# Releasing a group's row gathers in four runs of two instead of one run of eight

## The reference, cut to what matters

```
row, col = (edge_index[0], edge_index[1])
out = jnp.concatenate([x[row], edge_attr], axis=1)
out = jax.nn.selu(out @ W1a + b1a) @ W1b + b1b
summed = jax.ops.segment_sum(out, col, num_segments=x.shape[0])
counts = jax.ops.segment_sum(jnp.ones((out.shape[0],), out.dtype), col, num_segments=x.shape[0])
mean = summed / jnp.maximum(counts, 1.0)[:, None]
h = jnp.concatenate([x, mean, u[batch]], axis=1)
return jax.nn.selu(h @ W2a + b2a) @ W2b + b2b
```

## Time and profile before

| what | value |
|---|---|
| median of three runs | 3514.62 us (3498.83 to 3517.24) |
| the profiled execution | 3513.92 us, span 3512.1 us |
| mean granted TensorE clock | 0.782 of full speed |
| busy share: PE, PEld, DVE, ACT, POOL | 67%, 47%, 44%, 29%, 52% |
| DMA queue of POOL (q0) | 54240 packets, 57.23 MB, 7.5% of 16 engines |
| chain that ended last, by kind | PE 36%, another core or an unknown queue 25%, issue 22%, DVE 6%, ACT 5% |

### The profile page before, as it was taken

How to read it: one execution, slowest core, us unless ns; L and a number is a source line. 1 busy time by engine, 2 the same in 40 slices (tenths; PEclk the granted TensorE clock), 3 DMA queues, 4 the chain that set the end, 5 groups by cost and what they waited for, 6 DMA issues and landing times.

```text
span 3512.1 us, 52018 instructions
## 1 busy us (share of the span) xinstructions
PE 2340.6 (67%) x18382; PEld 1666.3 (47%) x18382; DVE 1547.9 (44%) x3098; ACT 1005.2 (29%) x2255; POOL 1824.9 (52%) x1853
## 2 busy tenths in 40 slices
PE   3999999787888862565656566565656656564643
PEld 1555565444444431454544455454545545453543
DVE  6899998233333441333433333343333334332333
ACT  4778776000000011222222222222222222222222
POOL 6366763555455557454444545444554544455552
PEclk9999999888888875677777777777767777676566
DMA  6658877649455521322222222222222222221111
GB/s 227 196 196 241 224 210 253 175 119 219 143 173 176 176 68 40 83 48 44 46 48 43 48 46 48 44 46 48 43 48 46 48 44 46 48 42 42 39 37 34
DMA packets 478172, 346.45 MB, mean 99 GB/s; under 512 B 357844, under 2 KB 428687, under 8 KB 474253
## 3 DMA queue, kind: packets, MB, share of 16 engines
q1 hardware_dynamic: 367443, 272.49, 27.4%
q0 software_dynamic: 54240, 57.23, 7.5%
q10 hardware_dynamic: 56250, 13.52, 1.9%
HBM read 200.58 MB, written 142.39 MB: 98 GB/s over the span
## 4 chain that ended last, share of the span: by engine, by line
PE 36%; another core or an unknown queue 25%; issue 22%; DVE 6%; ACT 5%; DMA 2%; SPq 2%; DVEq 1%; ACTq 1%; POOL 0%; POOLq 0%
PE agg_ps L1533 5%; PE u_ps L1664 4%; PE cnt_ps L1404 4%; PE cnt_ps L1625 3%; PE agg_ps L1410 3%; PE agg_ps L1411 3%; PE u_ps L1660 2%; PE agg_ps L1674 2%; PE agg_ps L1633 2%; ACT A_sb L1071 2%; PE t_ps L1617 1%; PE v_ps L1650 1%; DVEq L2192 1%; ACT A_sb L1217 1%
## 5 line engine op out<-in xcount | busy, mean ns | idle before, releaser
L976 POOL DMA_INDIRECT A_sb<-source_terms,src_cur x1172 | 1118.5, 954 | 1048.4 <-ACT src_cur L1203 718.1
L927 POOL DMA_INDIRECT sorted_edges<-pm_row,pm_to x440 | 482.7, 1097 | 338.8 <-DVE pm_to L1981 215.5
L1664 PE MATMUL u_ps<-arena 128*128 128x64 bf16 x3399 | 253.4, 212 | 385.5 <-issue 385.2
L1533 PE MATMUL agg_ps<-A_sb,arena 128*128 128x448 f16 x1911 | 426.1, 373 | 68.7 <-issue 65.7
L1857 DVE TENSOR_TENSOR arena<-iota_code,arena 128x2048 f16<-128x2048 f16 (+1 forms) x392 | 438.3, 1186 | 33.5 <-PE cnt_ps L1404 31.2
L1071 ACT ACTIVATE A_sb<-cnt_ps 128x392 f32 (+1 forms) x784 | 386.0, 499 | 123.4 <-PE cnt_ps L1404 73.0
L1664 PEld LDWEIGHTS u_ps<-arena 128*128 128x128 bf16 x3399 | 196.7, 110 | 439.9 <-issue 431.9
L2194 DVE TENSOR_TENSOR A_sb<-A_sb,agg_ps 65x48 f32 (+1 forms) x290 | 78.0, 269 | 728.7 <-remote 624.4
L1533 PEld LDWEIGHTS agg_ps<-A_sb,arena 128*128 128x128 bf16 x1911 | 189.5, 101 | 274.0 <-issue 133.0
L1404 PE MATMUL cnt_ps<-arena 128*128 128x98 f16 x3136 | 282.2, 214 | 31.2 <-ACT A_sb L1071 23.2
L1633 PE MATMUL agg_ps<-A_sb 128*65 128x48 f32 x2344 | 210.9, 250 | 131.4 <-issue 73.4
(11 more groups left out here) (308 smaller groups left out, 3379.3 us busy)
## 6 DMA issues: line engine op xcount, KB each, us to landing
counts_matrix<-A_sb SPq DMA_DIRECT2D x14, 5488.0 KB
A_sb<-counts_matrix SPq DMA_DIRECT2D x12, 5488.0 KB
arena<-in_edge_attr_dram SPq DMA_DIRECT2D x96, 256.0 KB
sorted_edges<-zrow SPq DMA_DIRECT2D x11, 1716.0 KB
A_sb<-source_terms,src_cur POOLq DMA_INDIRECT x1172
arena<-sorted_edges SPq DMA_DIRECT2D x143, 128.0 KB
overlapping_rows<-A_sb SPq DMA_DIRECT2D x1, 13056.0 KB, 39.4
A_sb<-in_edge_attr_dram SPq DMA_DIRECT2D x50, 256.0 KB
```

The lines of the kernel that those rows point to most:

```text
L927: pool.indirect_dma_start(out=sorted_d, out_offset=bass.IndirectOffsetOnAxis(ap=pm_to[:, k, j:j + 1], axis=0), in_=pm_row[:, k, j, :], in_ ...
L976: pool.indirect_dma_start(out=gath[k][:, j * F:(j + 1) * F], out_offset=None, in_=p_d, in_offset=bass.IndirectOffsetOnAxis(ap=src_cur[k][: ...
L1533: ins = pe.matmul(agg_ps[:, 0:SBN], Hsb[:, part, blk, :], Asb(half)[:, blk, :], start=False, stop=(part == 2), skip_group_check=True)
L1664: ins = pe.matmul(u_ps[:, j * F:(j + 1) * F], lane_p[u % 2][:, a, j * P:(j + 1) * P], P3[:, 2 * b + a, part, :], start=False, stop=(part = ...
```

## The change

POOL still issues the same 8 gathers for a group, from the same indices into the same buffer, and in the same order. But now it issues them in four runs of two, and waits ahead of each:

1. as before, for `z_made` of group g-6 and `idx_made` of group g;
2. for `attr_turned` of group g-4, which PE turns in slot g-6;
3. for `seg_ready` of group g-6: the window sums of slot g-6, the last thing PE does in that slot apart from units;
4. for `z_made` of group g-5, the DVE's next `add_terms`.

The last group has half the width and so gets four runs of one gather. The first six groups stay as they were.

```diff
-            def gather(g, k, width=EJ):
-                for j in range(width):
+            def gather(g, k, first=0, end=EJ):
+                for j in range(first, end):
                     pool.indirect_dma_start(
...
                 pool.wait_ge(z_made, g - DEEP + 1)
                 pool.wait_ge(idx_made, g + 1)
                 pool.sem_inc(pool_at, 1)
-                gather(g, k, width)
+                gather(g, k, 0, width // 4)
+                pool.wait_ge(attr_turned, g - DEEP + 3)
+                pool.sem_inc(pool_at, 1)
+                gather(g, k, width // 4, width // 2)
+                pool.wait_ge(seg_ready, g - DEEP + 1)
+                pool.sem_inc(pool_at, 1)
+                gather(g, k, width // 2, 3 * width // 4)
+                pool.wait_ge(z_made, g - DEEP + 2)
+                pool.sem_inc(pool_at, 1)
+                gather(g, k, 3 * width // 4, width)
```

## The result

The changed kernel takes 3286.14 us (median of 4 runs, 3275.39 to 3290.11), the kernel before 3515.93 us beside it (4 runs, 3498.83 to 3527.1). The ratio is 0.9346, 95% interval 0.93 to 0.9391.

The account below looks back on a forecast made before the run. The prediction took the edge stage as bound by gather bursts and the engines' work, which hardly overlap. From 3513.9 us, -46 for 112 slots and -16 for the last slots gave 3452 us; own range 3405 to 3495, 8 in 10 3310 to 3600.

Parts of the forecast that it names:

- What holds everything back: Edge stage: bursts of gathers slow all other engines, from 63% of the free pace in 3 us to 8% late.
- the shared-interface reading: DVE and GpSimd contend for SBUF interfaces, so the loss would lie inside DVE's instructions, however the gathers are cut.
- The 6 us more of slow time for a group cut in four: Estimate from the skill's fixed DMA cost of about 2.0 us; the prediction's own rows gave 3 x 0.85.
- Added waits at 0: POOL's three new waits a group: satisfied ones cost nothing; others, restarting 0.83 us after the event, also counted 0.
- The cut: Edge stage: how the runs merge; a period's 32 gathers, before in bursts of 8, 8, 16, become 4, 8, 8, 12.
- The price of the cut: Edge stage: slow time less work done in it makes a period 59.85 us, 1.65 less; -46 us over 28 periods.
- all as eights: Middle case of the finer cuts: every burst 8 gathers, 58.6 us a period, 25.4 in the last slots; 3405 us.
- The term for the last slots: Last slots: 16 gathers cut as 4 and 12, period 26.65 us, 1.65 less; -16 us over 9.5 pairs.
- Fine cut: Edge stage: runs pace themselves and stay apart; all fours 3307 us, all pairs 3279; 0.24 for anything below 3400.
- Serial: Between runs: engines find queues empty and work at 34% in short runs; all pairs 3693 us; chance 0.16.
- Bursts grow: Edge stage: releases chain groups into two bursts of 16 a period, +2.9 us each; 3595 us; chance 0.10.
- nothing changes: Edge stage: waits already past and bursts unchanged, or loss goes by number of gathers alone; 3514 us; chance 0.14.

Follow-up runs that it names:

- e7: Changed kernel with one gather in each of the four runs, so half the gathers; single run, 2542.05 us.
- e9: Changed kernel with plain loads of the same size in place of gathers, issued by POOL with the same waits; single run, 2318.84 us.
- e16: Changed kernel with gathers of 64 rows in place of 128, on a chip with the slow time; single run, 3289.87 us.
- e1: Changed kernel with one run of eight gathers per group, released by the window sums of six groups back; 3369.65 us, ratio 0.9686 to the kernel before.
- e13: The changed kernel itself, run again where the kernel before takes 3525.64 us; 3285.05 us, ratio 0.9346.
- e14: Changed kernel with two runs: two gathers at the turned attributes, six at the window sums; 3280.67 us, ratio 0.9336 to the kernel before.
- e3: Changed kernel with one run of eight per group, released by the turned attributes of four groups back; 3383.88 us, ratio 0.973 to the kernel before.
- e5: Changed kernel with two runs: two gathers at the window sums, six at the next terms; 3360.69 us, ratio 0.9675 to the kernel before.
- e2: Changed kernel with one run of eight per group, released by the next group's terms on DVE; 3474.63 us, ratio 0.9988 to the kernel before.
- e15: Changed kernel with two runs: four gathers at the turned attributes, four at the window sums; 3243.72 us, ratio 0.9209 to the kernel before.
- e10: Changed kernel with two gathers at the turned attributes, six at the window sums, on the chip without slow time; ratio 0.9999 to the kernel before.
- e11: Changed kernel with four gathers at the turned attributes, four at the window sums, on the chip without slow time; ratio 1.0003 to the kernel before.
- e8: Changed kernel with plain loads of the same size in place of gathers, issued by SyncE; single run, 2645.68 us.

## Why the prediction was wrong

**What holds everything back: right.** Gathers, and neither their bytes nor transfers as such: e7, e9, e16. The widest DVE operation still takes 947 to 959 ns (944 to 958 in the earlier trace rows), so the loss doesn't lie inside it. That operation has one input in PSUM; none with both inputs in SBUF was timed, and for such a one the shared-interface reading stays untested. The 6 us more of slow time for a group cut in four did not show: 13.66 us a slot in the changed kernel against 14.45 in e1.

**Added waits at 0: right for those already satisfied.** e13 and e14 differ by two waits a group and by 4 us, inside their intervals. For the others I took POOL's restart as 0.83 us after the event, but that event came in a free stretch. Behind a burst it is 4.9 us (2227.26 to 2232.20): POOL's own wait is held back like everyone's. I had not seen that.

**The cut: the step that failed.** "So I expect the 32 gathers of a period as 4, 8, 8 and 12." Measured: 8, 8, 8, 2 and 6. I argued from the events' distances in one free slot, and let the runs merge to 12 where POOL is behind. Up to slot 120 they don't merge beyond 8 in the changed kernel, nor in e1, e3, e5 and e14. A wait that is seen late only in a gap would do this, but e2 and the kernel before merge to 16 in spite of it, and so do the last slots; why one release caps the bursts and another doesn't stays open.

**The price of the cut: the term that was mis-sized.** By my own rates 8, 8, 8, 8 should take 58.6 us a period; e1 measured 57.8, so the rates hold for whole bursts. (The work in a burst of 8, 4.2, has the 27% up to its end; with the 8% after 9 us that the longer bursts have it is 3.9, and the period 59.3.) The price of "all as eights", 3405 of 3514 us, is e1's ratio, 0.969, but by luck in its parts: it counts eights in the last slots too, where most of e1's bursts are of 16.

The cut 8, 8, 8, 2, 6 gives, by the same formula, slow 3 x 10.85 + 3.35 + 8.35 = 44.25, worked 12.6 + 2.0 + 3.5 = 18.1, period 58.1. So a period should have lost 61.5 - 58.1 = 3.4 us. It lost 61.5 - 54.6 = 6.9, and 28 periods (at the unrounded 6.87) make the 192 us of the result, where the forecast was 46. Measured by e1 (on another chip, where e2 with its bursts of 16 has 61.1), the cap at 8 is 3.7 of these, and the split of the fourth burst is 57.8 - 54.6 = 3.2 where my sum had 0.5.

The rates add up busy time as if any work would do. What stands in the slot with two unit steps is a chain, PE to ACT to DVE to PE, and a pause or a short run lets its links through where the late part of a burst lets none. PE's clock, which is lower behind a long pause, may be a part of it. This is my reading; the runs show the sizes, not the shares of these causes. The term for the last slots was too small as well: -16 us, measured -32 for all behind slot 120.

**Rivals.** "Fine cut" had the size (3279 to 3307 us) by another cut, all pairs or all fours, which never appear. "Serial" is refuted by the time. On the pace in short runs, below 45% by its account, e15 has the second four at the free pace and the first four at 0.45 of 1.18, 38%, but there PE was busy for 91% of the time. "Bursts grow" and "nothing changes" did not occur, though e2 shows how near the latter was: with one release, by the event next to e1's, the burst of 16 stays. What I gave to everything below 3400, 0.24, was too little: the earlier trace rows against the earlier trace rows already had a factor of 7 between the early and the late pace.

**Signs.** POOL's idle time ended by turns and sums: seen in the count of gathers, while the profile names "remote" and "issue". A shorter PE issue time: seen. A shorter wait of ACT for `u_ps`: no, it grew, from 486.2 + 293.9 = 780 us in 1700 (by PE and by "remote") to 893.3 + 115.9 = 1009 in 1500. 14.8 us a slot: 13.66. Bursts of 4 and 12: no. DVE's widest operation as long as before: yes.

## What to carry to other kernels

Where every engine waits at once and for nothing that the profile names, lay the GpSimd timeline over the others: indirect gathers can hold back the events between engines and PE's own next matmuls, at a cost that follows their number and not their bytes. Then try to release them in short runs, so that a pause falls into the dependent chain. Two releases did as much as four, and whether there was such a pause was worth 3%; which events give it had to be tried, for no theory here foretold all the runs. Check first on the chip at hand that the effect is there: on one chip two such cuts were worth nothing.

## What was not expected of the hardware

**The same kernel takes 2639 us on one chip and 3474 to 3526 us on others.** The kernel before: 3478.62 and 3474.28 us on two chips, 3525.64 later on the second of these, 3514.62 ahead of the prediction, and 2638.61 us on a third chip, within 0.5% in 19 runs. TensorE's granted clock is higher there, 0.88 against 0.74 between 1300 and 2300 us (e10, e13), but PE isn't the bound at either: it is busy for 778 and 669 of those 1000 us. What is gone is the waiting for "remote" events. In e10 the stages ahead of the edges, which use an indirect store, end at 1169 us instead of 1317 to 1352, so it isn't the gathers alone. e10 and e14 are the same kernel, 2638.84 and 3280.67 us. What in a chip or its state makes the difference stays open, and the changed kernel itself was not run there; e10 and e11 stand for it.

**Events arrive late, all together.** In the burst shown ACT, SP and POOL resume 2.7 to 3.7 us after the start of the last gather, with 4.9 and 6.4 us between an event and its being seen; late in a burst DVE and ACT stand still. PE pauses between matmuls that wait for no event, 77 us in 700, and not at all with plain loads (e8, e9) or on the third chip (e10), so it isn't the events alone. What the gathers share with both was not found.

**The cost follows the number of gathers, and more than in proportion.** 64 or 128 rows, in as many packets: 13.66 us a slot. 4 or 8 gathers a slot: 8.42 and 13.66 us. Plain loads of the same bytes from POOL's queue: 7.20 us. The two cases with fewer or no gathers are single runs, and PE's higher clock in them, 0.97 and 0.98 against 0.77, may be a part of the difference.
